# Transposes of gathered rows moved beside the sums over d and the last MLP step, and gathers dealt evenly over the blocks

## What is computed

```
x0 = e                                   # (1024, 32, 16): rows gathered from 32 tables
xk = x0
for W in (W0, W1, W2):                   # (32, 32 or 64, 64)
    xk = relu(einsum('bmd,bhd,mhk->bkd', x0, xk, W))
    outs.append(sum(xk, axis=2))         # the sum over d
h = concatenate([outs..., dense_ctx])    # 192 + 16
h = maximum(h @ W_top1 + b_top1, 0)      # 512
h = maximum(h @ W_top2 + b_top2, 0)      # 256
y = h @ W_top3                           # 1
```

## Time and profile before

| | |
|---|---|
| median of 3 runs | 632.04 us (631.09 to 632.07) |
| the profiled execution's own time | 630.55 us |
| its span in the trace | 628.7 us |
| busy PE, DVE | 594.6 us (95%), 585.8 us (93%) |
| busy POOL, ACT | 443.2 us (70%), 355.5 us (57%) |
| granted TensorE clock, mean | 0.98 |

### The profile page before, as it was taken

One profiled execution on the slowest core, in us unless ns is written; L12 is line 12 of the kernel. 1 busy time (PEld: TensorE's weight loads), 2 busy tenths in 40 slices (PEclk: granted clock), 3 DMA queues, 4 the chain that ended last, 5 costly groups with the idle time before them and its releaser, 6 DMA issues.

```text
span 628.7 us, 8924 instructions
## 1 busy us (share of the span) xinstructions
PE 594.6 (95%) x3046; PEld 243.0 (39%) x3046; DVE 585.8 (93%) x398; ACT 355.5 (57%) x665; POOL 443.2 (70%) x305
## 2 busy tenths in 40 slices
PE   4398998999999999999999999999999999999988
PEld 4252332234343354334443354334443354334434
DVE  4759999999999989999999999999999999999873
ACT  0173754729394663829385574829385674829361
POOL 5767887888888884988878887988878460806120
PEclk9579999999999999999999999999999999999999
DMA  6899989994997689695999779795999789690000
GB/s 176 192 236 271 210 249 210 274 211 113 252 264 183 137 248 214 205 218 128 238 218 246 154 231 213 230 217 129 221 216 258 155 247 217 212 213 17 2 0 1
DMA packets 60175, 119.82 MB, mean 191 GB/s; under 512 B 15271, under 2 KB 33734, under 8 KB 60054
## 3 DMA queue, kind: packets, MB, share of 16 engines
q1 hardware_dynamic: 49414, 114.69, 73.7%
q0 software_dynamic: 7584, 1.96, 3.8%
q10 hardware_dynamic: 3152, 2.86, 1.7%
HBM read 115.27 MB, written 5.25 MB: 192 GB/s over the span
## 4 chain that ended last, share of the span: by engine, by line
PE 53%; POOL 21%; DVE 12%; issue 7%; ACT 3%; SPq 2%; DMA 1%; DVEq 0%; ACTq 0%; POOLq 0%
PE acc L968 47%; POOL emb L447 12%; POOL z_pool L472 8%; DVE z_dve L529 8%; PE psm L1071 2%; SPq L426 2%; PE psm L1079 2%; DMA x_rot<-in_tbl_dram 1%; DVE z_dve L549 1%; DVE x0b L698 1%; PE acc L983 1%; ACT xq L717 1%; ACT xq L725 1%; ACT xq L771 1%; PE psm L1086 1%
## 5 line engine op out<-in xcount | busy, mean ns | idle before, releaser
L529 DVE TENSOR_TENSOR z_dve<-xq,x0b 128x2048 f32<-128x2048 f32 x179 | 398.5, 2279 | 12.4 <-ACT xq L717 7.5
L968 PE MATMUL acc<-z_dve,w_cin 128*64 128x512 f32 x1688 | 387.2, 597 | 9.9 <-DVE z_dve L529 7.1
L472 POOL TENSOR_TENSOR z_pool<-x0b,xs 128x2048 f32<-128x2048 f32 x45 | 205.3, 4565 | 89.4 <-ACT xs L717 88.9
L447 POOL DMA_INDIRECT emb<-in_tbl_dram,ids_all x224 | 218.3, 974 | 66.3 <-issue 61.3
L968 PEld LDWEIGHTS acc<-z_dve,w_cin 128*64 128x64 f32 x1688 | 127.3, 136 | 230.5 <-issue 166.9
L754 ACT ACTIVATE xq<-acc 64x512 f32<-64x512 f32 x64 | 36.5, 570 | 123.1 <-PE acc L968 122.4
L968 PE MATMUL acc<-z_pool,w_cin 128*64 128x512 f32 x360 | 85.0, 593 | 1.4 <-POOL z_pool L472 1.3
L549 DVE TENSOR_TENSOR z_dve<-xq,x0b 128x1024 f32<-128x1024 f32 x64 | 75.8, 1215 | 6.9 <-ACT xq L754 5.0
L717 ACT ACTIVATE xs<-acc 64x512 f32<-64x512 f32 x124 | 73.4, 592 | 1.7
L771 ACT ACTIVATE xq<-acc 32x512 f32<-32x512 f32 x128 | 72.2, 564 | 1.9
L725 ACT ACTIVATE xq<-acc 32x512 f32<-32x512 f32 x128 | 72.2, 564 | 1.7
(11 more groups left out here) (99 smaller groups left out, 241.8 us busy)
## 6 DMA issues: line engine op xcount, KB each, us to landing
x0b<-x0t SPq DMA_DIRECT2D x120, 512.0 KB, 13.2
x_rot<-x0t SPq DMA_DIRECT2D x60, 512.0 KB
x_rep<-x0t SPq DMA_DIRECT2D x15, 512.0 KB, 7.9
x0b<-x0t SPq DMA_DIRECT2D x16, 256.0 KB, 8.1
emb<-in_tbl_dram,ids_all POOLq DMA_INDIRECT x224
x0t<-emb_t SPq DMA_DIRECT2D x28, 128.0 KB
w_cin<-in_L_rec_W_dram SPq DMA_DIRECT2D x16, 64.0 KB
x_lo<-x0t SPq DMA_DIRECT2D x15, 64.0 KB
```

Of the source, the lines that this page charges most:

```text
L447: nc.gpsimd.indirect_dma_start(out=rows[:, D * f:D * f + D], out_offset=None, in_=tables[f], in_offset=bass.IndirectOffsetOnAxis(ap=ids_al ...
L472: nc.gpsimd.tensor_tensor(z_pool[:, n % ZP_SLOTS, :, :], x0b[b % 2][:, 2 * j:2 * j + 2, :], xs[l - 1][:, :].unsqueeze(1).broadcast_to([P, ...
L529: nc.vector.tensor_tensor(z_dve[:, base % Z_SLOTS, :, :], in0.unsqueeze(1).broadcast_to([P, 2, N]), in1, ALU.mult).then_inc(z_made, 1)
L968: ins = nc.tensor.matmul(acc[l][K * side:K * side + K, :], weights[c], z[:, c, NH * side:NH * side + NH], start=start and c == 0, stop=sto ...
```

## The change

It does four things. PE's transposes for half 1 of the next tile go, in half 0 of tiles 1 to 6, from between layer 0 and layer 2 to between the fourth pair of layer 2 and `sum_d`. Those for half 0 of the tile after next go, in half 1, from behind the fifth pair of layer 2 to behind the seventh, where `mlp3` follows. ACT's copies follow them: in half 0 from ahead of `x1_pool` to behind `zsum_out`, in half 1 from ahead of `y_out` to behind it. The waits of PE for these copies move to the next instructions that write over them (`sum_d` no longer waits for the copy, `mlp1` does; `mlp3` waits for none). And `gathers(b)` becomes 21 in block 0 and 16 in every block from 1 on, as long as there are any; before it was 22, 19, 17, 18, 18, 11 in blocks 0 to 5 and 16 in the later ones.

```diff
     def gathers(b):
 
-        return {0: (14, 2, 6), 1: (6, 8, 5), 2: (5, 7, 5), 3: (5, 8, 5), 4: (5, 8, 5), 5: (1, 5, 5)}.get(b, (5, 6, 5))
+        return (14, 2, 5) if b == 0 else (5, 6, 5)
...
                     x2_swp(t, k)
-                    if k == 0 and not first_tile and not last_tile:
-                        move_half(t + 1, 1)
                     if not last:
                         x1_pool(t, k + 1)
...
                         if not first_tile:
                             zsum_out(t - 1)
+                            if not last_tile:
+                                move_half(t + 1, 1)
...
+                    if k == 1 and not first_tile:
+                        y_out(t - 1)
                     if k == 1 and more:
                         move_half(t + 2, 0)
-                    if k == 1 and not first_tile:
-                        y_out(t - 1)
...
-                    if not first_tile:
-                        if k == 0 and not last_tile:
-                            transpose_half(t + 1, 1)
-                        if k == 1:
-                            mlp2(t - 1)
+                    if not first_tile and k == 1:
+                        mlp2(t - 1)
...
                         if i == 3 and k == 0 and not first_tile:
                             if not last_tile:
-                                pe.wait_ge(emb_copied, 2 * (t + 1))
+                                pe.wait_ge(emb_copied, 2 * t + 1)
+                                transpose_half(t + 1, 1)
                             sum_d(t - 1)
-                        if i == 4 and k == 1 and more:
-                            if first_tile:
-                                pe.wait_ge(emb_copied, 2)
-                            else:
-                                pe.wait_ge(h2_relu, t)
-                            transpose_half(t + 2, 0)
-                        if i == 6 and k == 1 and not first_tile:
+                        if i == 6 and k == 1:
                             if more:
-                                pe.wait_ge(emb_copied, 2 * (t + 1) + 1)
-                            mlp3(t - 1)
+                                if first_tile:
+                                    pe.wait_ge(emb_copied, 2)
+                                else:
+                                    pe.wait_ge(h2_relu, t)
+                                transpose_half(t + 2, 0)
+                            if not first_tile:
+                                mlp3(t - 1)
...
                         if k == 0:
+                            if not last_tile:
+                                pe.wait_ge(emb_copied, 2 * (t + 1))
                             mlp1(t - 1)
                         else:
                             pe.wait_ge(y_copied, t)
-                    elif k == 1:
-                        pe.wait_ge(emb_copied, 3)
```

## The result

Measured beside each other on one chip, four executions each: before 631.57 us (630.90 to 632.07), changed 637.44 us (637.38 to 638.34), ratio 1.0084 with a 95% interval of [1.0059, 1.0110]. The change costs 5.9 us by the medians. The profiled execution took 637.41 us and its span is 635.5 us, 6.8 us more than before's. The prediction was 633.7 us with a range up to 635.4: the sign was right, the size was a third of what came.

A forecast was written before the change was run, and what follows sets the result against it. The prediction took DVE's few waits as the clock, with PE and ACT chains lacking slack in half 0. Moves +3.2 and gathers -1.5 gave +1.7 us on before's median 632.04, so 633.7 us, range 631.2 to 635.4.

The forecast's parts named there:

- Half-0 transposes: Tiles 1 to 6: transposes between pool pair and sums over d delay PE's chain 0.53 us per tile, +3.2 us.
- ACT's wait for L1062: Sign in half 0: ACT's wait for PE's sums over d grows from 0.7 to about 1.5 us.
- the L771 waits of 0.28: Sign in layer 2 of half 1: DVE's 0.28 us waits for ACT vanish in six tiles of seven.
- Half-1 transposes: Half 1, moved behind the seventh pair: PE's saving and ACT's delay reach no wait of DVE, zero.
- SP's queue: Half 0: the later copy delays SP's x0t write and following loads, but x_rep lands in time; zero, by 2 to 6 us.
- The gathers: Block 4: two gathers fewer each in blocks 3 and 4 make POOL's layer-2 product timely, removing DVE's excess wait, -1.5 us.
- The sign that POOL would wait for xs in block 3 too: With fewer gathers ahead of its layer-2 product, POOL would wait for ACT's xs in blocks 3 and 4.
- Late loads: Rival: x_rep or x_rot lands 14 us after issue, DVE waits 1 us or more per tile; 636 or more, chance 0.05.
- The gathers give nothing: Rival: POOL still comes last in block 4, so only +3.2 stands; 635.2 us, chance 0.10.
- Half hidden: Rival: transposes beside the sums cost PE only about 0.3 us per tile, total +0.3; 632.3 us, chance 0.22.
- faster: Rival: half-0 transposes and copy hide in existing waits, only the gathers' 1.5 us gain remains; 630.5 us, chance 0.13.
- slower: Whole kernel: outcome slower than before, chance given as 0.37 + 0.10 + 0.05, rounded to 0.51.

The follow-up runs named there:

- e2: The changed kernel with the old gathers of the kernel before, so only the moves: 636.43 us, ratio 1.0076.
- e3: The kernel before with only the half-0 move of transposes and copy: 636.35 us, ratio 1.0074.
- v5: f1 with half-0 transposes behind layer 2's second pair, ACT's copies and half-1 transposes as before: ratios 0.9923 and 0.9884 to the kernel before.
- e4: The kernel before with only the half-1 move of transposes and copy: 632.03 us, ratio 1.0008.
- f1: The changed kernel with one gather fewer in block 0, run on three chips (f1_again is a repeat): ratios 0.9914, 0.9945 and 0.9930 to the kernel before.
- e1: The kernel before with the new even gathers alone, no moves: 650.96 us, ratio 1.0313.
- after_again: The changed kernel itself, unaltered, timed again on another chip; two such repeats took 647.22 and 647.13 us, which one is not stated.
- f2: The changed kernel with three gathers more in block 0 (24 in place of 21): 650.29 us, ratio 1.0069 to the kernel before.
- v1: The kernel before with the sums over d moved to the transposes' old place ahead of layer 2, ACT's copies ahead of x1_pool: 644.41 us, 1.0008.
- v3: v1 with 16 gathers in block 4 and 13 in block 5: 642.15 us, ratio 0.9986 to the kernel before.

## Why the prediction was wrong, point by point

**Half-0 transposes, +3.2 us: right in the traces, at 3.1.** The working held row by row; the medians of e2 and e3 say 4.5 and 4.4 us, and the prediction has no term for the rest. Timelines of PE's weight loads and of ACT in the changed kernel, tile 4:

```profile
365.92 0.20 PEld L968 LDWEIGHTS acc<-z_dve,w_cin 128*64 128x64 f32 x4 [1.14 <-DVE z_dve L529]
...
369.50 0.20 PEld L1056 LDWEIGHTS psm<-ident,emb 128*128 128x128 f32 x2 [0.81 <-issue]
369.87 0.41 PEld L1062 LDWEIGHTS psm<-zacc,sel 128*64 128x64 f32 x6 [0.17 <-issue]
```

```profile
370.56 0.27 ACT L827 COPY zsum<-psm 128x128 f32<-128x128 f32 x1 [1.67 <-PE psm L1062]
...
370.88 0.37 ACT L822 COPY emb_t<-psm 128x256 f32<-128x256 f32 x1
371.28 4.59 ACT L725 ACTIVATE xq<-acc 32x512 f32<-32x512 f32 x8
```

PE still has its 1.14 us of waiting at 365.92, and the gap ahead of the transposes is the 0.81 us of the earlier trace rows. From PE's pair to the copy of zsum it is 370.56 - 365.92 = 4.64 us; in the earlier trace rows it was 364.75 - 360.63 = 4.12: 0.52 later, 0.53 predicted. ACT's wait for L1062 is 1.67 us (I wrote 1.5), DVE's 1.27 (1.28), in five tiles 1.24 or 1.27; the L771 waits of 0.28 went. e3 shows the half-0 move alone gives the same 1.27. The Trainium skill (TensorEngine Tiling (Array Packing), Key Properties) states that a change of the tiling mode drains TensorE; the 0.81 us fit it. In v5 the same 0.81 us stand ahead of the transposes and a tile takes 70.70 us against before's 70.65: the gap costs next to nothing where PE waits anyway.

**Half-1 transposes, 0: right** within the noise (e4, 1.0008 [0.9994, 1.0022]).

**SP's queue, 0: right for DVE, not for POOL.** SP issued x_rep at 373.82 in tile 4, 3.3 us later against DVE's first product of layer 1 than before; ACT's copy of it waited for DVE and not for the load, 15 times. SP's timeline, and the view of waits:

```profile
373.82 0.55 SPq L376 DMA_DIRECT2D x_rep<-x0t  x1
```

```profile
ACT xq L780 <- DVE z_dve L529: 68.7, 15, 6.5
...
POOL z_extra L478 <- DMA x_hi<-x0t: 9.5, 3, 6.5
```

`x_hi`, which the prediction names in the queue but does not price, did come late: POOL waited 9.5 us for it in three places, the longest 6.54 us at 526.94, where before has one wait of 2.0 us. e3 has 10.0 us of it and e4 3.7, so it comes mostly with the half-0 move. POOL had slack there: no wait of DVE's follows, and from 518.31 to 588.70 the tile takes 70.39 us.

**The gathers, -1.5 us: the step that failed.** Its first half held: POOL's product of block 4 waits for ACT (at 215.46, idle 1.11 us ahead of it; the estimate was 213.9 to 214.0), and the 1.98 us fell to 1.27. But the step went on: "No later block gets more than 16 gathers except block 12 ..., which still has fewer than a steady block", and so no loss behind block 4. It priced every gather at 1.25 us. One, the 127th, cost 8.9 us (7.99 idle and 0.94 busy, so 7.7 more than the usual 1.25). In before it went without a stall and had 7 us of slack behind it. The rows that I took show blocks 4 and 8 alone; block 5 was not read. Block 5 went from 11 gathers to 16, five of them new ones ahead of POOL's product, and I counted only that 16 is a steady block's load. Priced as the prediction prices them, those five cost 6.2 us and would just have fitted into the 7.03 us; it is the stall that did not fit. f1_again has the same six gathers ahead of its product, unheld, and POOL there still waits 1.48 us for ACT. Even so block 5 was the place to read, since there above all the change adds gathers. The stall made the product late (256.98), and DVE lost 4.1 us in the next block. Undone by one gather, the changed kernel gets 5 to 7 us faster (f1, on the slower chips). Why POOL stands there at all stays open, as said above. The sign that POOL would wait for xs in block 3 too did not come: there it waited 1.28 us for a load of x0b.

**The start.** About 1.1 us of the span lie ahead of 52 us, where the prediction had nothing. 0.6 of it, ahead of 47 us, is also in e1 (which has only the gathers) and e3 (only the half-0 move) and not in e2, so it follows neither edit. The wait of 0.45 to 0.82 us for x0b at 52 us stands in the three kernels with the half-0 move (changed, e2, e3) and in none of the other three on that chip; one profile each, and no instruction ahead of it differs on DVE. Whether the change causes it is open.

**The rivals.** Late loads (636 or more) came nearest in number and was not the cause: behind 52 us DVE waited for no load, and ACT's copy of x_rep for none either; x_hi alone was late, for POOL, which had slack. In `after_again`, though, x_rot was late by 4.75 us, so on that chip this rival came true once. "The gathers give nothing" was wrong about block 4. Half hidden and faster are out, as DVE's wait is 1.27 us. In the chances, slower should be 0.52 and faster 0.13, not 0.51 and 0.14.

## What to carry to other kernels

Where small work of another tile is put is decided by the wait that it displaces, to half a microsecond: the same two transposes cost 0.5 us per tile behind the fourth pair and 0.05 behind the second, where PE waits for DVE. A deal of background transfers is not only a load per block: read for each block that gets more of them what slack stands behind, and look for single long idle times of the issuing engine with no releaser, by their number in the run. Two edits that look independent (when rows are gathered, when they are read) should be tried one by one: the even deal alone cost some 19 us, with the later transposes 2.6 by the traces (4.1 less 1.5) and 1.4 by the medians (5.9 less 4.5). And a kernel tuned on one chip should be timed on others: one gather fewer in block 0 made a kernel that is faster than before on three chips, and its likely gain, in block 1, is one that the first chip does not show.

## What the runs showed of the hardware

- POOL was held 7.9 to 8.3 us at its 127th indirect DMA of 128 rows in all six traces in which the one before stands right ahead of it, with two gathers under way (f2) as with five; no other of the 237 stood over 1.4 us there without a releaser. In 15 of the 18 traces the 127th starts 1.2 to 2.2 us after the last packet of the 126th, so work put in between hides the hold (idle 3.6 us and less); in three (before, e4, v1) it starts ahead of that packet. It is in all kernels the same gather, so count and gather are not parted. The Trainium skill (DMA: Bandwidth & Descriptors, SWDGE vs HWDGE vs iDMA) states that GpSimd's DMAs write their descriptors into rings in SBUF. A ring that comes round at that count would fit, but no run here shows it.
- Chips differ more than the change: before took 632 us in the first two comparisons and 643 to 646 us on three other chips. In the traces of the others the first of DVE's products with x0b comes at 50 to 56 us in place of 47 (9.2 to 11.8 us of idle time ahead of it in place of 7.5 to 7.7). A wait of 4.4 to 5.8 us in block 1, as v1 and v3 show it, would be about the rest; the kernel before was profiled on the first kind only.
- On two of those chips the changed kernel was 0.2 and 0.5% slower than before (the 0.2% within its interval of no change), on the first kind 0.84%.
